# Filling of the expert queues issued by ScalarE in place of the sync engine, in an attention and mixture-of-experts kernel

## The reference

```python
x = x + attention(layernorm(x), ctx)        # 16 heads of 8, rotary positions, window of 64 keys back, softmax
x = x + moe(layernorm(x))                   # all 4096 tokens together
# moe: logits = x @ router; two experts of 8 per token, gates from their softmax;
# a token's place in an expert's queue is the count of earlier pairs of that expert,
# places past the capacity of 1281 are dropped;
# each expert: silu(queue @ w1) @ w2; the two results of a token are weighed, added, and added to x
```

## Time and profile before

| | |
|---|---|
| median of three runs | 603.98 us (603.66 to 605.69) |
| the profiled execution | 607.17 us |
| its span in the trace | 605.0 us |
| TensorE busy | 423.4 us (70%) |
| GpSimd busy | 376.0 us (62%) |
| VectorE busy | 343.2 us (57%) |
| ScalarE busy | 263.5 us (44%) |
| moved by DMA | 70.51 MB, mean 117 GB/s |
| queue fillings (L311) | 8 DMAs of 682.5 KB, median 7.3 us from issue to landing |
| filling of the dump rows (L317) | 1 DMA of 672.0 KB, 6.6 us |

### The profile page before, as it was taken

How to read it: one execution, slowest core, us unless ns; L and a number is a source line. 1 busy time by engine, 2 the same in 40 slices (tenths; PEclk the granted TensorE clock), 3 DMA queues, 4 the chain that set the end, 5 groups by cost and what they waited for, 6 DMA issues and landing times.

```text
span 605.0 us, 16774 instructions
## 1 busy us (share of the span) xinstructions
PE 423.4 (70%) x5554; PEld 330.8 (55%) x5554; DVE 343.2 (57%) x1071; ACT 263.5 (44%) x578; POOL 376.0 (62%) x392
## 2 busy tenths in 40 slices
PE   3365678888988888879878610896959678695610
PEld 2244456666766666657656400785748466584500
DVE  4772447686888888877857531572734526353210
ACT  1112235544545554445545301886546564573400
POOL 5531114566777777775756764057878687687874
PEclk9995789898999999898989755898778796896955
DMA  9887675668877878777763335242544435342322
GB/s 187 216 216 177 173 175 160 171 127 164 173 162 165 187 163 165 145 151 152 175 127 42 44 58 117 76 98 26 107 94 41 96 31 104 62 35 20 33 22 21
DMA packets 89616, 70.51 MB, mean 117 GB/s; under 512 B 9632, under 2 KB 76448, under 8 KB 89056
## 3 DMA queue, kind: packets, MB, share of 16 engines
q1 hardware_dynamic: 68576, 60.36, 38.8%
q0 software_dynamic: 20992, 9.53, 18.5%
HBM read 39.11 MB, written 31.00 MB: 116 GB/s over the span
## 4 chain that ended last, share of the span: by engine, by line
POOL 35%; issue 26%; SPq 14%; DMA 11%; PE 9%; ACT 1%; DVE 1%; POOLq 1%; DVEq 0%; ACTq 0%
POOL out L1302 17%; POOL queues L1205 10%; PE bank L455 7%; DMA maxima_scratch<-maxT 6%; SPq L354 3%; SPq L334 3%; SPq L352 2%; SPq L339 2%; POOL rest L1256 2%; POOL qk L1253 1%; DMA k_pack<-k_scratch 1%; POOL base L1228 1%; DVE ys L1144 1%; DMA k_scratch<-parts 1%; ACT parts L799 1%
## 5 line engine op out<-in xcount | busy, mean ns | idle before, releaser
L1302 POOL DMA_INDIRECT out<-ys,row_token x88 | 140.9, 1601 | 55.7 <-issue 34.9
L874 DVE TENSOR_REDUCE maxima<-bank 128x4 f32<-128x512 f32 x128 | 87.5, 686 | 67.1 <-PE bank L455 65.8
L1205 POOL DMA_INDIRECT queues<-rows,index x64 | 100.9, 1577 | 19.8 <-issue 19.8
L743 ACT ACTIVATE probs<-bank 128x512 f32<-128x512 f32 x128 | 76.4, 597 | 81.7 <-PE bank L455 81.1
L455 PE MATMUL bank<-xTp,w1p 128*128 128x512 f32 (+1 forms) x288 | 76.5, 424 | 6.9 <-DVE xTp L1120 6.9
L455 PE MATMUL bank<-q_pack,k_pack 128*128 128x64 bf16 x1024 | 55.0, 199 | 34.9 <-DMA q_pack<-maxima_scratch 32.5
L845 ACT ACTIVATE hid<-bank 128x512 f32<-128x512 f32 (+1 forms) x96 | 52.2, 543 | 47.0 <-PE bank L455 40.4
L1167 DVE TENSOR_TENSOR hidp<-hid,hidp 128x512 fp32r<-128x512 f32 (+1 forms) x96 | 56.8, 602 | 23.5 <-ACT hidp L849 20.6
L455 PEld LDWEIGHTS bank<-xTp,w1p 128*128 128x128 f32 x288 | 57.4, 226 | 20.5 <-issue 5.5
L455 PE MATMUL bank<-k_pack,q_pack 128*64 128x128 bf16 x1024 | 56.6, 238 | 16.1 <-DMA k_pack<-k_scratch 14.8
L455 PEld LDWEIGHTS bank<-q_pack,k_pack 128*128 128x128 bf16 x1024 | 39.2, 101 | 49.0 <-DMA q_pack<-maxima_scratch 31.9
(11 more groups left out here) (107 smaller groups left out, 713.1 us busy)
## 6 DMA issues: line engine op xcount, KB each, us to landing
k_pack<-k_scratch SPq DMA_DIRECT2D x64, 192.0 KB, 3.9
q_pack<-q_scratch SPq DMA_DIRECT2D x64, 128.0 KB, 3.2
queues<-empty SPq DMA_DIRECT2D x8, 682.5 KB, 7.3
xs<-queues SPq DMA_DIRECT2D x8, 650.0 KB
q_scratch<-parts SPq DMA_DIRECT2D x16, 192.0 KB
k_scratch<-parts SPq DMA_DIRECT2D x16, 192.0 KB
xin<-in_x SPq DMA_DIRECT2D x16, 128.0 KB, 3.5
cin<-in_ctx SPq DMA_DIRECT2D x16, 128.0 KB, 3.4
```

What stands on the lines that cost most here:

```text
L743: nc.scalar.activation(probs[u % 2][:], bb[u % 2][:], ACT.Exp).then_inc(S["prob_s"], 1)
L874: v.reduce_max(maxima[par][:, 4 * hg:4 * hg + 4, i2], ab[u % 2][:].rearrange("p (h c) -> p h c", c=P), AX).then_inc(S["max_s"], 1)
L1205: g.indirect_dma_start(queues, bass.IndirectOffsetOnAxis(ap=index[par][:, n:n + 1], axis=0), rows[par][:, n // TILES, n % TILES, :], None, ...
L1302: g.indirect_dma_start(out, bass.IndirectOffsetOnAxis(ap=row_token[par][0:n, t:t + 1], axis=0), ys[s][0:n, col // P, :], None, compute_op= ...
```

## The change

The function that issues queue fillings, the wait for `init_made`, the filling of the dump rows and the first two fillings go from SP's program to the head of ScalarE's, and the fillings at the end of SP's steps -2 to 1 go to the end of ScalarE's steps -2 to 1. The transfers themselves, their sizes and their semaphores stay.

```diff
@@ SP's program @@
-            def empty_queues(first, last):
-                for e in range(first, last):
-                    sp.dma_start(queues[e * QUEUE:(e + 1) * QUEUE, :].rearrange("(p r) c -> p r c", p=INIT_P),
-                                 empty[:]).then_inc(S["init_out"], 16)
             load_context(1, 1)
-            sp.wait_ge(S["init_made"], 1)
-            sp.dma_start(out[ALL:ALL + QUEUE, :].rearrange("(p r) c -> p r c", p=INIT_P),
-                         empty[:, :, 0:DIM]).then_inc(S["dump_out"], 16)
-            empty_queues(0, 2)
-            REST_OF_QUEUES = [(2, 4), (4, 6), (6, 7), (7, 8)]
...
                 pack(k + 2, par, 2)
-                if isinstance(k, int) and -2 <= k < LOOP:
-                    empty_queues(*REST_OF_QUEUES[k + 2])
@@ ScalarE's program, ahead of its steps @@
+            def empty_queues(first, last):
+                for e in range(first, last):
+                    act.dma_start(queues[e * QUEUE:(e + 1) * QUEUE, :].rearrange("(p r) c -> p r c", p=INIT_P),
+                                 empty[:]).then_inc(S["init_out"], 16)
+            act.wait_ge(S["init_made"], 1)
+            act.dma_start(out[ALL:ALL + QUEUE, :].rearrange("(p r) c -> p r c", p=INIT_P),
+                         empty[:, :, 0:DIM]).then_inc(S["dump_out"], 16)
+            empty_queues(0, 2)
+            REST_OF_QUEUES = [(2, 4), (4, 6), (6, 7), (7, 8)]
...
                     nc.scalar.copy(parts[:, 1, :, :], rest[:]).then_inc(S["part2"], 1)
+                if isinstance(k, int) and -2 <= k < LOOP:
+                    empty_queues(*REST_OF_QUEUES[k + 2])
```

## The result

Ten runs of the changed kernel gave a median of 609.53 us (606.34 to 613.13), ten of the kernel before on the same chips 605.34 us. The ratio is 1.0083 with a 95% interval of 1.0045 to 1.0122, so the change costs 5.0 us, between 2.7 and 7.4. The forecast was +2.9. The profiled execution took 611.14 us, with a span of 609.0, 4.0 more than the profiled one of before.

What follows compares the result with a forecast made beforehand. SP's queue was taken to bound the kernel from 22 us to near 155 us, where GpSimd's scatters take over. Terms +6.6 - 1.0 + 0 - 1.5 - 1.2 = +2.9 us gave 606.9 us; range 596.5 to 611.5.

Steps and rivals of the forecast that it cites:

- term A: Start: the first three fillings, issued earlier on ScalarE, delay the constants and so the first matmul; +6.6 us, bounds 0 to 8.3.
- (B): Step -2, two fillings: SP freed, but bytes set the stretch, not the issue; -1.0 us, bounds 0 and -4.3.
- (C): Step -1, two fillings: SP freed, but the small maxima wait behind the fillings; 0, bounds -5.5 and +1.0.
- (D): Step 0, one filling: SP reaches its scratch writes sooner, the filling runs beside them; -1.5 us.
- (E): Step 1, one filling: SP reaches its scratch writes sooner, the filling runs beside them; -1.2 us.
- (F): ScalarE's issuing in steps -2 and -1: hidden under its waits; 1.2 us at most if step -2's cover is gone.
- even shares: Rival: engines share by bytes, or constants proceed while fillings wait; start +3.9 or less, sum -6, 598 us; chance 0.29.
- full relief: Rival: no loss at the start, steps -2 to 1 give most of their bounds; -10, 594 us; chance 0.08.
- Strict turns: Rival: queues served in turn without overlap; start +8.3, step -1 +1.0, sum +5.6, 609.6 us; chance 0.12.
- ScalarE is held as SP was: Rival: ScalarE's step -2 issues take 2.2 us each, delaying its copy 2.9 us; with the start some +6, 610; chance 0.06.

## Why the prediction was right

The direction, slower, was right, and 609.5 lies in the range. It was not right for the reason given, and the size of term A is in part luck. The prediction named two signs of being wrong, and both came: the constants landed before 10 us (at 9.1), and ScalarE's first fillings took over 1 us each to issue (2.1). For the first it said: "then A is the failed term and the time is under 602". A did fail as written, but the time wasn't under 602, because another load was late by enough to make up for it. Of the signs of being right, the first scratch writes (29.12) and the later maxima came; SP's packing issues were not back at 0.5 to 0.6 us (2.87, 2.38 and 2.47), and the steps from 103.19 on were not those of before. By terms:

- **(A)** predicted +6.6, measured +7.1. The size was right, and two of its steps were not. The carrier: "TensorE's first matmul waits for that [...] so a delay of the constants passes through whole". The constants were 0.8 us late, batch 1's x 9.2 (statistics at 18.96 against 9.74). I costed only the load that the chain of before waited for, and not the ones behind it that had slack then. The mechanism: rows served in turn. The filling's rows, which were to begin near 4.4 us, began at 9.2, and a third of their length moved SP's transfers by 0.4 to 0.5 us. What held is that what is issued ahead of a transfer stands ahead of it, and so the sum of the three fillings, 8.3 us less an overlap; that the slack that x had (it was 9.2 late, and 7.1 of that was felt) and my division by 1.26 come to nearly the same is luck. In the sum itself the dump rows were misread: they are 1344 pieces of 512 bytes, not long rows, and of the 428 GB/s in 16 to 17 us two thirds are the first rows of a filling, not theirs.
- **(B)** predicted -1.0, measured -3.0. "The bytes set this stretch, not the issue" was too strong: in this step fillings beside the scratch writes cost less than those ahead of them. But those writes are the first thing of step -1, and were held there.
- **(C)** predicted 0 between -5.5 and +1.0, measured +3.1, outside the bounds. The mechanism was as described and came to +0.3: 5.4 us lost at the maxima, behind two fillings, and 5.0 won behind them. What the term left out is that step -2's fillings would run into this step's scratch writes, +2.7. B and C together are 0.0, where -1.0 was predicted.
- **(D), (E)** predicted -1.5 and -1.2, measured -1.4 and -0.7.
- **(F)** ScalarE's issues of 1.12 to 1.15 us for two are hidden, as said. At the start they took 4.86 us, in an engine with nothing to do; its first copy is at 10.80 where that was 10.05, with the constants.

Together -2.0 for B to E, by sum -3.7 predicted. Behind them step 2 is 1.4 us longer than before (103.19 to 123.31, against 98.20 to 116.96), where the same period was predicted: the last filling, issued at 101.25, meets that step's first scratch writes, which take 4.39 us to issue in place of 2.56. So step 1's filling wins nothing either, once what it leaves to the next step is counted (-0.7 + 1.4). The first scatter is at 123.80 against 116.85, 7.0 us late; of this 2.3 come back in the step behind it (141.27 - 123.31 = 17.96 us against 20.26 of before, in which the two maxima took 4.2 and 4.0 us to land). That step differed by as much between other kernels with the same program there, so I take it for what varies from run to run. The medians differ by 0.8%, 5.0 us, in place of 7.0. That such a shift carries whole to the end is therefore not shown to better than 2 to 3 us.

Of the rivals, *even shares* and *full relief* fall with the start, which is 7.1 us longer. *Strict turns* has the total that lies nearest (609.6, against 606.9 of the forecast), but not by its terms: its start of 8.3 is further from 7.1 than my 6.6. The rule that it shares with term A, single rows in turn, is refuted. The sentence of the Trainium skill ("DMA: Bandwidth & Descriptors", Queues, rings and completion order) on packets in turn is neither shown nor refuted: the trace records single rows, and not how many of them an engine takes as one packet. *ScalarE is held as SP was* is true at the start (4.20 us for the two fillings) and in no later step; its total, 610, is as near as that of strict turns.

## What to carry to other kernels

Before a DMA is moved to another engine's queue, ask when it will be issued there: a queue in which nothing waits ahead of it is not a gain if its bytes then land ahead of loads that were first before. Here a second hardware queue gave no right of way on the DMA engines, and SP was held at its issues even so; where its transfers ran without a gap, a filling cost the same wherever it was put. So look at the price of the transfer first: the fillings went twice as fast from 96 or more partitions as from 64. Moved and widened the kernel was faster than the kernel before; with the widening alone, or the later move alone, no difference could be told.

## What was not expected of the hardware

A DMA that reads a tile of 64 partitions shows a DMA share of 1.00 at 210 GB/s, while the same bytes from 112 go at 413 and the same share. A full share therefore doesn't say that the engines are at their rate. And SP was held at its issues in the changed kernel (1.74 to 2.33 us each, from 4.90 to 11 us, where the same took 0.45 to 0.62 before) when the only thing new were the DMAs in ScalarE's queue; what is full then, the trace doesn't say.
